# Eight-batch conditioned attention block on one core: VectorE's copies between SBUF tiles become second evictions from PSUM or move to ScalarE and GpSimd, and the order is written anew

## The reference, cut to what matters

```python
# block 0 (per batch element): graph attention over the first M = 20 tokens
row_zero = x.sum(-1) == 0
q_exp = where(row_zero[..., None], 0.0, cond[:, None, :])
self_feat = concat([x, q_exp]) @ W_self.T + b_self
for d in range(2):
    A = adj (or adj transposed)[:, :, :20, :]          # 11 int labels
    aff = (self_feat @ Wq.T + bq) . (kv @ Wk.T + bk) / sqrt(16)
    aff = where(A.sum(-1) > 0, aff, -9e15) + (A @ w_bias + b_bias)
    output += (softmax(aff) @ kv) @ Wout + bout
x = x + relu(output)
# block 1: transformer layer, 16 heads of 16
nx = x * rsqrt(mean(x * x) + 1e-5) * w_norm1 * (1 + scale1) + shift1
q, k, v = nx @ wq, nx @ wk, nx @ wv                    # q and k rotated
x = x + softmax(q k^T / 4) v @ wo + bo
nx = the same norm with w_norm2, scale2, shift2
return x + (gelu(nx @ w_gate) * (nx @ w_up)) @ w_down  # 1024 hidden
```

## Time and profile before

| | us |
|---|---|
| median of 3 runs | 541.65 (538.02 to 543.03) |
| the profiled execution | 537.04 |
| its span, first to last instruction | 535.3 |
| TensorE busy | 462.3, 86% of the span |
| VectorE busy | 360.1, 67% |
| GpSimd busy | 250.5, 47% |
| ScalarE busy | 240.3, 45% |
| TensorE's mean granted clock | 0.939 of full speed |

### The profile page before, as it was taken

How to read it: one execution, slowest core, us unless ns; L and a number is a source line. 1 busy time by engine, 2 the same in 40 slices (tenths; PEclk the granted TensorE clock), 3 DMA queues, 4 the chain that set the end, 5 groups by cost and what they waited for, 6 DMA issues and landing times.

```text
span 535.3 us, 10092 instructions
## 1 busy us (share of the span) xinstructions
PE 462.3 (86%) x3728; PEld 396.3 (74%) x3728; DVE 360.1 (67%) x617; ACT 240.3 (45%) x458; POOL 250.5 (47%) x210
## 2 busy tenths in 40 slices
PE   3675856778898899999998999989799979999997
PEld 3573744666677589788977898869687967787896
DVE  1676896899899729972998398559952792661321
ACT  1233422332732594248534863363546426537422
POOL 3254776385645833454575366316563351240232
PEclk9765865989999899999999999999989999999999
DMA  7902336612350150142115312141014003300000
GB/s 137 371 0 63 92 118 186 135 40 86 125 97 1 62 167 26 40 111 90 31 41 109 101 56 75 28 140 45 0 46 134 23 2 114 125 4 6 16 21 20
DMA packets 35231, 41.30 MB, mean 77 GB/s; under 512 B 5872, under 2 KB 27888, under 8 KB 35056
## 3 DMA queue, kind: packets, MB, share of 16 engines
q1 hardware_dynamic: 35184, 40.67, 26.5%
HBM read 29.90 MB, written 10.49 MB: 75 GB/s over the span
## 4 chain that ended last, share of the span: by engine, by line
PE 52%; DVE 24%; DMA 7%; issue 7%; POOL 6%; ACT 2%; SPq 2%; POOLq 0%; DVEq 0%; ACTq 0%
PE ps L2131 24%; PE ps L2349 6%; PE ps L2364 5%; DVE nm L1615 4%; PE ps L2324 4%; PE ps L2249 3%; PE ps L2174 3%; DMA nzb<-nz_d 3%; PE ps L2261 2%; PE ps L2233 2%; DMA nz_d<-nz 2%; DVE xr L1568 2%; SPq L333 2%; DVE ya L1568 1%; POOL aff L628 1%
## 5 line engine op out<-in xcount | busy, mean ns | idle before, releaser
L2131 PE MATMUL ps<-splz,wh 128*128 128x256 f32 x512 | 97.0, 287 | 1.7 <-ACT g L1036 0.7
L1615 DVE TENSOR_REDUCE nm<-ps 128x2 f32<-128x512 f32 x128 | 83.4, 680 | 13.9 <-PE ps L2324 13.9
L999 ACT ACTIVATE ex<-ps 128x512 f32<-128x512 f32 x128 | 70.3, 597 | 33.4 <-PE ps L2349 31.9
L2131 PEld LDWEIGHTS ps<-splz,wh 128*128 128x128 f32 x512 | 79.5, 191 | 5.4 <-issue 2.9
L595 POOL TENSOR_TENSOR hs<-g,hs 128x512 fp32r<-128x512 f32 x32 | 41.1, 1289 | 81.5 <-ACT hs L1046 81.5
L2131 PE MATMUL ps<-splz,wl 128*128 128x256 f32 x256 | 72.3, 282 | 0.0
L1665 DVE TENSOR_TENSOR g<-ps,g 128x512 f32<-128x512 f32 x32 | 22.0, 686 | 51.3 <-PE ps L2131 41.2
L2324 PE MATMUL ps<-kst,qst 96*128 96x256 f32 x256 | 51.8, 305 | 5.3 <-DVE nm L1615 4.3
L2131 PE MATMUL ps<-wh,hs 128*128 128x256 f32 x256 | 53.1, 288 | 0.9 <-POOL hs L595 0.7
L2349 PE MATMUL ps<-qst,kst 100*128 100x256 f32 x256 | 49.5, 306 | 3.3 <-ACT ex L999 1.6
L2349 PEld LDWEIGHTS ps<-qst,kst 100*128 100x128 f32 x256 | 36.2, 191 | 17.1 <-ACT ex L999 11.3
(11 more groups left out here) (129 smaller groups left out, 1020.7 us busy)
## 6 DMA issues: line engine op xcount, KB each, us to landing
...
```

The source lines that it names most:

```text
L999: act.activation(ex[:, h % EXR], ps[:, h % 2].rearrange("p (c s) -> p c s", c=TC), ACT.Exp, scale=SCALE).then_inc(ex_ok.sem, 1)
L1615: dve.tensor_reduce(nm[:, :, h], ps[:, h % 2].rearrange("p (c s) -> p c s", c=TC), AX.X, ALU.max, negate=True).then_inc(mx_ok.sem, 1)
L2131: ins = pe.matmul(dst, lhs(a, k), rhs(c, k), start=first_ and n == 0 and m == 0, stop=last_ and n == len(ks) - 1 and m == 2, **kw)
```

## The change

The results are to be the same; what computes them changes.

- **Two evictions in place of an eviction and a copy.** `selfc`, `qkadd` and `aadd32` now add twice from PSUM: once into the rounded high tile, once into the whole. `selfh` is gone. GpSimd's `low` waits for both.
- **Norms.** The 1/256 goes into `square` as a scale (RMS = 1/16). Epsilon is added by GpSimd, in `pow1` and `pow2`. `xr_scaled` and `xr2_scaled` move to ScalarE. `nxc` and `nzc` move from ScalarE to VectorE, `nxh` and `nzh` from VectorE to ScalarE.
- **Block 0.** `mask` moves to GpSimd, as four instructions in place of three. The comparison that makes `nz` moves to GpSimd (`nonzero`).
- **Maxima.** `nmx` is gone. `nmT` transposes the 16 whole columns; ScalarE evicts the high part (`nrowc`), and VectorE's new `nlow` subtracts that from PSUM.
- **Waits.** PE's steps that come in pairs or in fours (`selfm`, `q0`, `qk`, `v`, `wo`, `gate`, `up`, `down`, `affm`) wait only in the first; some waits that follow from others are left out.
- **Order.** All five lists are written anew.

```diff
-        nm = sb("nm", [P, TC, H])
-        nm4 = sb("nm4", [P, TC, 2, 2, PAIRS], F32R)
+        nm = sb("nm", [P, TC, 2, PAIRS])
-        nrow = ex[0:4 * PAIRS, EXR - 1, 0, :]
+        nrow = ex[0:H, EXR - 1]
...
+            def nonzero(b):
+                pool.wait_ge(rs_ok.sem, rs_ok.at(b))
+                before(pool, nz_out, b - 1)
+                pool.tensor_scalar(nz[:], rs[:], 0.0, 0.0, ALU.is_equal, ALU.is_equal).then_inc(nz_ok.sem, 1)
...
             def selfl(b):
                 pool.wait_ge(selfh_ok.sem, selfh_ok.at(b))
+                pool.wait_ge(self_ok.sem, self_ok.at(b))
                 low(splx[:, 1], self32[:], splx[:, 0], selfl_ok)
+
+            def mask(b):
+
+                pool.wait_ge(adj_ok.sem, adj_ok.at(b))
+                before(pool, am_ok, b - 1)
...
+                pool.tensor_scalar(mf, cnt, 0.0, SCALE, ALU.is_gt, ALU.mult).then_inc(mul_ok.sem, 1)
+                pool.tensor_scalar(of, cnt, 0.0, NEG, ALU.is_le, ALU.mult).then_inc(off_ok.sem, 1)
+                pool.tensor_scalar(ws, ws, wb[:, L:L + 1], None, ALU.add).then_inc(off_ok.sem, 1)
+                pool.wait_ge(off_ok.sem, off_ok.at(b))
+                pool.tensor_tensor(of, ws, of, ALU.add).then_inc(msk_ok.sem, 1)
...
             def pow1(b):
+                pool.wait_ge(ss1_ok.sem, ss1_ok.at(b))
+                pool.tensor_scalar(v1[:], ss1[:], EPS, None, ALU.add).then_inc(v1_ok.sem, 1)
                 pool.wait_ge(v1_ok.sem, v1_ok.at(b))
                 pool.tensor_tensor(r1[:], v1[:], mhalf[:], ALU.pow).then_inc(r1_ok.sem, 1)
...
-                    act.activation(xr[:, c], x[:, c], ACT.Square, accum_out=ss1[:, c:c + 1]).then_inc(ss1_ok.sem, 1)
+                    act.activation(xr[:, c], x[:, c], ACT.Square, scale=RMS, accum_out=ss1[:, c:c + 1]).then_inc(ss1_ok.sem, 1)
+
+            def scaled(dst, r, r_ok, ok):
+                def step(b):
+                    act.wait_ge(r_ok.sem, r_ok.at(b))
+                    x = res[b % RES]
+                    for c in range(TC):
+                        ins = act.activation(dst[:, c], x[:, c], ACT.Copy, scale=r[:, c:c + 1])
+                    ins.then_inc(ok.sem, 1)
+                return step
+
+            def nxh(b):
+                act.wait_ge(nx_ok.sem, nx_ok.at(b))
+                before(act, qk_ps, b - 1)
+                before(act, v_ps, b - 1)
+                act.activation(sply[:, 0], nx32, ACT.Copy).then_inc(nxh_ok.sem, 1)
...
-                act.activation(nrow.bitcast(F32R), ps[0:4 * PAIRS, BANK["nmT"], 0:S], ACT.Copy).then_inc(nrow_ok.sem, 1)
+                act.activation(nrow[:, 0, :].bitcast(F32R), ps[0:H, BANK["nmT"], 0:S], ACT.Copy).then_inc(nhigh_ok.sem, 1)
...
-                dve.tensor_tensor(self32[:], ps[:, BANK["self"]].rearrange("p (k s) -> p k s", k=KC), self32[:], ALU.add).then_inc(self_ok.sem, 1)
-
-            def selfh(b):
-                dve.wait_ge(self_ok.sem, self_ok.at(b))
-                high(splx[:, 0], self32[:], selfh_ok)
+                whole = ps[:, BANK["self"]].rearrange("p (k s) -> p k s", k=KC)
+                dve.tensor_tensor(splx[:, 0], whole, self32[:], ALU.add).then_inc(selfh_ok.sem, 1)
+                dve.tensor_tensor(self32[:], whole, self32[:], ALU.add).then_inc(self_ok.sem, 1)
...
-                    whole = qkl[:, 2 * n:2 * n + 2]
-                    dve.tensor_tensor(whole, ps[:, BANK["qkT"][n]].rearrange("p (k s) -> p k s", k=KC), rbT[:, 2 * n:2 * n + 2, :],
-                                      ALU.add).then_inc(qk_ok.sem, 1)
-                    dve.wait_ge(qk_ok.sem, qk_ok.at(b, n + 1))
-                    dve.tensor_copy(qkh[:, 2 * n:2 * n + 2].bitcast(F32R), whole).then_inc(qkh_ok.sem, 1)
+                    src, bias = ps[:, BANK["qkT"][n]].rearrange("p (k s) -> p k s", k=KC), rbT[:, 2 * n:2 * n + 2, :]
+                    dve.tensor_tensor(qkh[:, 2 * n:2 * n + 2].bitcast(F32R), src, bias, ALU.add).then_inc(qkh_ok.sem, 1)
+                    dve.tensor_tensor(qkl[:, 2 * n:2 * n + 2], src, bias, ALU.add).then_inc(qk_ok.sem, 1)
...
+            def nlow(b):
+
+                dve.wait_ge(nhigh_ok.sem, nhigh_ok.at(b))
+                dve.tensor_tensor(nrow[:, 1, :].bitcast(F32R), ps[0:H, BANK["nmT"], 0:S], nrow[:, 0, :], ALU.subtract).then_inc(nrow_ok.sem, 1)
...
-            def nzh(b):
-                dve.wait_ge(nz_sb.sem, nz_sb.at(b))
-                high(splz[b % 2][:, 0], nz32, nzh_ok)
+            def nzc(b):
+                dve.wait_ge(nz_ps.sem, nz_ps.at(b))
+                for k in range(KC):
+                    ins = dve.tensor_scalar(nz32[:, k, :], ps[:, BANK["nz"], k * S:(k + 1) * S], tab[:, 1, b, k:k + 1], tab[:, 1, b, 2 + k:3 + k],
+                                            ALU.mult, ALU.add)
+                ins.then_inc(nz_sb.sem, 1)
...
-                    pe.wait_ge(nxl_ok.sem, nxl_ok.at(b))
-                    if b == 0:
-                        pe.wait_ge(w_low["qk"].sem, w_low["qk"].at(0))
+                    if c == 0:
+                        if b == 0:
+                            pe.wait_ge(w_low["qk"].sem, w_low["qk"].at(0))
+                        pe.wait_ge(nxl_ok.sem, nxl_ok.at(b))
```

More of the change, by code:

```diff
@@ L354, in _ @@
             load_x(0)
-            weights("self", 0)()
+            weights("q0", 0)()
             load_xT(0)
-            cond()
-            get_vec()
-            nz_store(0)
-            get_wsk()
-            nz_load(0)
-            get_wsv()
-            weights("q0", 0)()
             get_consts()
             get_wb()
+            load_x(1)
+            nz_store(0)
+            weights("self", 0)()
+            cond()
+            load_adj(0)
+            nz_load(0)
+            nz_store(1)
@@ L415, in _ @@
-            k_stack(0, 32, 1)(0)
-            k_stack(1, 64, 1)(0)
+            weights("d", 2)()
+            q_stack(0, 0, 1)(0)
+            q_stack(0, 64, 1)(0)
+            q_stack(1, 32, 1)(0)
+            k_stack(0, 0, 1)(0)
+            weights("u", 3)()
+            weights("d", 3)()
+            k_stack(0, 32, 1)(0)
+            load_xT(3)
+            k_stack(1, 64, 1)(0)
+            nz_store(3)
+            nz_load(3)
             load_xT(4)
+            nrows(0)
             load_adj(3)
-            weights("u", 3)()
@@ L564, in _ @@
             nrows(7)
+            store(3)
+            store(4)
             store(5)
@@ L751, in _ @@
             pow1(2)
+            mask(3)
             aadd(0)(3)
@@ L1761, in _ @@
             mx(12)(0)
+            mx(13)(0)
             pTc(1)(2)
+            mx(14)(0)
+            mx(15)(0)
+            pTc(3)(2)
+            nlow(0)
             rot(0)(1)
-            pTc(3)(2)
-            mx(13)(0)
-            mx(14)(0)
+            yadd(2)
+            x1add(2)
             rot(1)(1)
-            yadd(2)
-            mx(15)(0)
-            nmx(0)
-            x1add(2)
-            wlow("u", 1)()
-            wlow("u", 2)()
+            wlow("u", 3)()
             selfc(3)
-            selfh(3)
-            wlow("u", 3)()
+            qkadd(0)(1)
+            qkadd(1)(1)
             kev(3)
@@ L1830, in _ @@
-            mask(4)
-            nzh(0)
+            nlow(1)
+            qkadd(0)(2)
+            qkadd(1)(2)
+            adjm(4)
             am(0)(4)
-            qkadd(0)(2)
+            hmul(0)(0)
             am(1)(4)
             amax(0)(4)
-            qkadd(1)(2)
+            amax(1)(4)
             asums(0)(4)
-            amax(1)(4)
-            hmul(0)(0)
-            xr_scaled(3)
             asums(1)(4)
-            hmul(1)(0)
             mx(0)(2)
             mx(1)(2)
-            pTc(1)(4)
+            hmul(1)(0)
@@ L1879, in _ @@
+            rowsum(5)
             qkadd(0)(3)
+            nlow(2)
             qkadd(1)(3)
+            hmul(0)(1)
+            hmul(1)(1)
             selfc(5)
-            selfh(5)
-            hmul(0)(1)
+            kev(5)
             vb(5)
-            mask(5)
-            kev(5)
-            hmul(1)(1)
-            v1_in(4)
             kb(5)
+            adjm(5)
             am(0)(5)
             am(1)(5)
-            amax(0)(5)
             mx(0)(3)
             mx(1)(3)
+            amax(0)(5)
@@ L1927, in _ @@
+            qkadd(0)(4)
+            nlow(3)
+            qkadd(1)(4)
             rowsum(6)
-            nzh(2)
-            nmx(3)
             yadd(5)
-            qkadd(0)(4)
-            qkadd(1)(4)
+            hmul(0)(2)
+            hmul(1)(2)
             x1add(5)
-            hmul(0)(2)
             adjm(6)
             selfc(6)
-            selfh(6)
-            mask(6)
+            vb(6)
             kev(6)
-            vb(6)
             kb(6)
-            hmul(1)(2)
-            am(0)(6)
@@ L2708, in _ @@
             st(7)(2)
-            gate(2, 0)(1)
-            affm(0)(5)
+            small(0)(5)
+            small(1)(5)
+            kT(5)
             st(8)(2)
@@ L2885, in _ @@
             st(7)(4)
-            small(1)(7)
-            small(0)(7)
+            gate(0, 0)(3)
```

(16 more changed lines are left out.)

1499 lines of the change are left out of this document (719 added, 780 removed).

## The result

The median is 512.59 us (511.35 to 513.04), against 539.84 us (537.36 to 543.03) for the kernel before in the same rounds: the ratio is 0.9495, with a 95% interval from 0.9452 to 0.9537. That is -27.2 us. The forecast was 526, a fall of 15.5 us, so the direction held, and 512.6 lies in the range; the size was missed by nearly half of what was gained. Some executions are over 1.5% slower than the fastest of the same kernel; medians are over all executions, ratios and their intervals leave these slow ones out.

The account below looks back on a forecast made before the run. Bound by a start of chained latencies, then a middle with TensorE 92% busy. Terms -14.5 + 0.4 + 2.2 + 1.4 (serial latencies) - 5.7 + 0.7 = -15.5: 537.0 to 521.5, 4.6 below the median, so 526; range 509 to 542.

Parts of the forecast that it names:

- VectorE -14.5, at 0.36 for each us: VectorE gets 40.6 us less work net; at 0.36 us of chain for each, 14.5 us less.
- ScalarE +0.4: Scalings and copies come, evictions go: net +10 us of ScalarE work at 0.045, +0.4 us (-1 to +3).
- ScalarE's slower start costs nothing there: In the serial latency of one norm, without hops, 3.2 us before and 2.8 after, so no cost from ScalarE.
- GpSimd +2.2: 56 small steps added to GpSimd at 0.3 us, 17 us at 0.13: +2.2 us (0 to 5.8).
- Order -5.7 and +0.7: New order: two waits in batch 0 go, -5.7 us; self weights fetched later at the start, +0.7 us (0 to 3).
- The two waits of the first batch: 2.90 us of second `amax` behind `rotated_bias`, 2.80 us of transposed weights' last eviction behind a copy; both were to go.
- steps exchanged among neighbours: TensorE's list in the rest: the old one but for such exchanges; no gain or loss priced.
- a gain of 0 to 3, taken at nothing: SyncE's `nrows(3)` no longer behind the load of nz of batch 6; counted as 0 us, since TensorE has gates to do.
- The start feeds on itself: Rival: half of the start's 37.8 us idle time goes and the clock rises: -30 us, 512; chance 0.17.
- The waiting moves on: Rival: VectorE's other steps inherit the waiting inside the removed ones, about -2 us, about 540; chance 0.18.
- GpSimd's queue: Rival: `am`, `aadd` and later GpSimd steps stand behind the mask; at half of 46 us, +7.5, 549; chance 0.10.
- The signs: Expected profile: VectorE near 320 us, PSUM sums 684 ns, TensorE idle near 29 us in first 100 us, 23 in the middle.

Follow-up runs that it names:

- f_scale: Kernel before, with only the 32 scalings of both norms moved from VectorE to ScalarE: 533.79 us, ratio 0.9875.
- d_dummy: New kernel plus 32 row sums of 128x256 on VectorE that nobody needs or waits for: 515.07 us, ratio 0.9564.
- b_mask: New kernel with the mask's three steps of each batch back on VectorE: 510.36 us, ratio 0.9461.
- e_steps: New kernel's steps, with every engine's list in the order of the kernel before: 547.91 us, ratio 1.006 to the kernel before.
- h_rest_old: New kernel's steps, in new order up to the first eviction of the maxima and in old order from there on: 539.96 us, ratio 1.0013.
- e_order: Steps of the kernel before, with the engines' lists in the new kernel's order: 541.8 us, ratio 1.0003.
- b_scale: New kernel with the 32 scalings of both norms back on VectorE: 529.4 us, ratio 0.9807.

## Why the prediction was right in its sign, and short in its size

**VectorE -14.5, at 0.36 for each us.** The work fell by 38.5 us (360.1 to 321.6) for 40.6 forecast: the prices were right but for the shift and scale, 0.54 for 0.42. The ratio held where one part was tried alone in the old order: f_scale gave -6.7 (-9.6 to -3.8) for -6.5. d_dummy's +3.7 for +4 is too uncertain to count for it. What failed is the use of one ratio for all steps in both orders. In after's order the scalings are worth 16.8 us, and they stand where TensorE waits; the mask, and the second sums in place of copies, are worth nothing that can be measured. In before's order all the steps together are worth nothing (+3.2).

**ScalarE +0.4** can't be tested at its size; its load rose by 4.7 us (245.0 for 240.3), where 10 were forecast. But "ScalarE's slower start costs nothing there" priced the scaling by its duration, 2.8 for 3.2 us a norm, without the time that it stands in VectorE's list. For the second norm that is the 1.0 us a batch.

**GpSimd +2.2.** The 56 small steps take 21.7 us for 17, the mask's 0.38 to 0.55 each, the other 24 0.22 to 0.31. What b_mask gained by taking the mask back (1.8 us, give or take 3.6) doesn't speak against that price. `am` did wait for the mask, 4.5 us, which was named as a sign that the forecast is wrong; it cost nothing that can be measured, so the sign was a bad one.

**Order -5.7 and +0.7.** This is the term that was mis-sized: -5.0 was forecast, and from e_steps to after, with the new steps in place, the order is worth -30.5 us. The two waits of the first batch are gone or short (the second is 0.83 us, of 2.80), but the new fetches delay VectorE's first sum by 2.7 us and not by 0.7, so that after leads before by 2.5 us at `x1add(0)`, and not by the forecast 5. The rest arises behind it. The old order costs some 12 us up to `nrowc(0)` and some 15 from `nrowc(1)` on. For both, the working says nothing beyond the two waits: for TensorE "steps exchanged among neighbours", for SyncE "a gain of 0 to 3, taken at nothing". The step about `nrows(3)` named a place that matters: alone on SyncE the old order costs 15.4 us. It was held for free because the trace of before shows no wait there. The wait only arises when all else is faster. What is late next was asked for each edit by itself, in before's timeline and not in the faster one.

**The sum** as a sum failed. The steps alone give +3 us, the order alone 0, both -27. The ratios gave -10.5 for the steps and -5 for the order, and -15.5 for both; only the third agrees in sign with what was measured. Adding up two parts of which neither brings anything alone, and landing on the right side, was luck.

**The rivals.** *The start feeds on itself* gave the time, but not the path. Its clock part is there (0.83 and 0.87 for 0.72 and 0.74). But half of the start's idle time was to go, and hardly any did (36.2 for 37.8), and h_rest_old, with after's start, ends where before does. *The waiting moves on* fits the times of each half alone: e_steps and e_order end at 540 us and over. *GpSimd's queue* is out by the result, and by b_mask, where it has no mask and nothing is gained that can be measured.

**The signs.** VectorE busy near 320: 321.6. Sums at 684 ns: 678 to 688. TensorE's idle time in the middle 23 us: 20.3. In the start 29: 36.2, wrong. VectorE's small steps under 0.45 us: met by all that run in every batch.

What stays open: which exchanges in the rest make up its 15 us, since the lists of the computing engines depend on each other and were not tried one by one; how much of the loss of e_steps and b_scale is the place of their moved steps; and, of the steps' 27.4 us in the new order, what the 10 or so beyond the scalings are. The new way of the maxima, the exchange of evictions and copies in the norms, the epsilon on GpSimd and the repeated waits left out on TensorE were not tried alone.
